# Products that keep TensorE at work across three stage boundaries, and two products moved ahead of a gate's, in a two-layer transformer kernel

## The reference

```python
x = x + ffn0(cond0(x, itok_B_0_8))   # adapter and layernorm chosen by language, then a quantised gated FFN
x = x + ffn1(cond1(x, itok_B_0_2))

def cond1(x, type_label):            # experts: one chosen by type, two shared
    s0, s1 = dense(x, swi[0], swo[0]), dense(x, swi[1], swo[1])
    eo = relu(x @ wi[type_label]) @ wo[type_label]
    gate_in = concatenate([eo[:, 0], s0[:, 0], s1[:, 0]])     # first token of each sequence
    w = softmax(relu(gate_in @ g1) @ g2)
    return eo * w[0] + s0 * w[1] + s1 * w[2]

def ffn1(x):                         # attention (16 heads), then a mixture of 8 experts, top 2
    x = x + attention(layernorm(x)) @ w_o + b_o
    h = layernorm(x)
    return x + mixture(h, top2(h @ gate_w + gate_b))
```

## Time and profile before

| | |
|---|---|
| median of 3 runs | 612.7 us (610.8 to 613.97) |
| the profiled execution | 612.18 us |
| its span, first to last instruction | 610.5 us |
| mean granted clock of PE | 0.966 |
| busy: PE, DVE, ACT, POOL | 536.3, 395.8, 375.2, 296.9 us |
| layer zero, typed experts, layer one begin on PE at | 2.36, 145.32, 216.72 us |

### The profile page before, as it was taken

How to read it: one execution, slowest core, us unless ns; L and a number is a source line. 1 busy time by engine, 2 the same in 40 slices (tenths; PEclk the granted TensorE clock), 3 DMA queues, 4 the chain that set the end, 5 groups by cost and what they waited for, 6 DMA issues and landing times.

```text
span 610.5 us, 18637 instructions
## 1 busy us (share of the span) xinstructions
PE 536.3 (88%) x5836; PEld 463.2 (76%) x5837; DVE 395.8 (65%) x1440; ACT 375.2 (61%) x799; POOL 296.9 (49%) x308
## 2 busy tenths in 40 slices
PE   6798998576999969899899998998988789999991
PEld 3555665366999958689788887887777688999991
DVE  5977788992433313367676876769866446668882
ACT  2366776884666523465546566466786477888870
POOL 1366777753000047442266836366476564555551
PEclk9999999997999969999999999999999799999996
DMA  8922999122333211020525202033322122236364
GB/s 280 376 48 77 400 401 392 57 73 82 107 104 102 77 39 40 23 53 20 170 51 183 71 20 59 20 74 83 78 63 59 50 75 64 72 89 197 86 195 134
DMA packets 75774, 70.81 MB, mean 116 GB/s; under 512 B 26802, under 2 KB 63012, under 8 KB 75300
## 3 DMA queue, kind: packets, MB, share of 16 engines
q1 hardware_dynamic: 67968, 55.34, 29.3%
q0 software_dynamic: 6400, 13.19, 6.6%
q10 hardware_dynamic: 1316, 1.15, 0.6%
HBM read 30.19 MB, written 39.46 MB: 114 GB/s over the span
## 4 chain that ended last, share of the span: by engine, by line
PE 44%; issue 6%; DVE 5%; POOL 5%; DMA 1%; DVEq 1%; ACT 1%; ACTq 0%; POOLq 0%
PE u_py L1712 7%; PE u_py L1874 6%; PE u_pz L1855 6%; PE u_pg L1855 3%; PE u_pf L1874 3%; PE u_pg L1755 2%; PE u_pz L1701 2%; PE u_pz L1703 2%; PE u_pz L1702 2%; PE u_pg L1763 2%; POOL rows_dram L1562 1%; PE u_pg L1777 1%; POOL u_eo_ew L1525 1%; PE u_pe L1727 1%; PE u_pf L1733 1%
## 5 line engine op out<-in xcount | busy, mean ns | idle before, releaser
L1572 POOL DMA_INDIRECT y_dram<-u_hh,v_to x71 | 68.1, 960 | 62.0 <-DVE u_hh L2645 49.7
L1562 POOL DMA_INDIRECT rows_dram<-u_row,u_slots x64 | 62.8, 981 | 46.8 <-DVE u_slots L2515 30.4
L1712 PE MATMUL u_py<-cwo,u_hh 128*128 128x128 f32 x512 | 68.5, 281 | 0.9 <-ACT u_hh L2097 0.7
L1712 PEld LDWEIGHTS u_py<-cwo,u_hh 128*128 128x128 f32 x512 | 63.5, 193 | 5.5 <-issue 2.5
L1874 PE MATMUL u_py<-w,v_h 128*128 x384 | 53.2, 282 | 7.1 <-DVE u_hh L2645 3.9
L1855 PE MATMUL u_pz<-v_xT,v_held 128*128 128x128 f32 x384 | 52.8, 283 | 4.8 <-DVE v_h L2625 4.2
L2097 ACT ACTIVATE u_hh<-u_pz 128x512 f32<-128x512 f32 x64 | 38.0, 596 | 28.0 <-PE u_pz L1703 25.0
L1874 PEld LDWEIGHTS u_py<-w,v_h 128*128 128x128 f32 x384 | 47.5, 194 | 9.9 <-issue 9.9
L1855 PEld LDWEIGHTS u_pz<-v_xT,v_held 128*128 128x128 f32 x384 | 48.2, 198 | 6.0 <-issue 4.7
L2170 ACT ACTIVATE v_held<-w 128x512 f32 x71 | 44.9, 633 | 11.8 <-PE u_pz L1855 3.6
L2177 ACT ACTIVATE v_h<-u_pz,p_bT 128x128 f32<-128x128 f32 x124 | 36.5, 368 | 12.4 <-PE u_pz L1855 10.4
(11 more groups left out here) (378 smaller groups left out, 1489.1 us busy)
## 6 DMA issues: line engine op xcount, KB each, us to landing
rows_dram<-zero SPq DMA_DIRECT2D x1, 17160.0 KB, 49.8
v_x<-rows_dram SPq DMA_DIRECT2D x71, 65.0 KB
w<-in_mw SPq DMA_DIRECT2D x2, 2048.0 KB
cwt<-in_cw SPq DMA_DIRECT2D x1, 2560.0 KB
xs_dram<-zero SPq DMA_DIRECT2D x1, 2240.0 KB, 12.6
e_xs<-xs_dram SPq DMA_DIRECT2D x35, 64.0 KB, 1.9
eo_dram<-e_y SPq DMA_DIRECT2D x35, 64.0 KB, 1.5
x_dram<-x SPq DMA_DIRECT2D x8, 256.0 KB
```

What stands on the lines that cost most here:

```text
L1562: pool.indirect_dma_start(rows_dram, bass.IndirectOffsetOnAxis(ap=slots[:, q, k, u:u + 1], axis=0), row[:, q, k, u, :], None).then_inc(sen ...
L1572: pool.indirect_dma_start(y_dram, bass.IndirectOffsetOnAxis(ap=vto[t % XR][:], axis=0), vy[:, t % XR, :], None).then_inc(v_sent[t % XR], 16)
L1712: last = nc.tensor.matmul(py[:, u * D:(u + 1) * D], hh[:, e % HR, u * P:(u + 1) * P], cwo[:, m * KF + k], start=(k == 0 and u == 0), stop= ...
```

## The change

In layer zero `first(2, 0)` and `first(2, 1)` stand ahead of `turn_rows(0)`; before, they stood between the first `up`s. At four places PE gets products whose results nobody reads: two of `zero` with 512 columns at the end of layer zero; three of the identity and typed weights with 256 columns at the start of the typed experts, into a bank that is written afterwards; two with 512 columns at their end; one with 512 columns in layer one, behind `turn_x(0)`. All are float32. In layer one `first(0, 0, 0)` and `first(0, 0, 1)` stand ahead of `gate(-1, 0)`, and `first(0, 0, 2)` ahead of `gate(-1, 1)`. In ScalarE's list `hidden(0, 0, 0)` stands ahead of its `gate(-1, 0)`. `gate` does nothing at any other i, and the order of the rest is the same.

```diff
                 second(1)
+                first(2, 0)
+                first(2, 1)
                 turn_rows(0)
                 up(0, 0)
-                first(2, 0)
                 up(0, 1)
-                first(2, 1)
                 first(2, 2)
...
                 turn_bias()
+                for n in range(2):
+                    nc.tensor.matmul(pg[:], zero[:, 0:P], zero[:, 0:INNER], start=True, stop=True)
...
+                def idle(bank, columns):
+                    nc.tensor.matmul(bank[:, 0:columns], ident[:], w1[:, 0:columns // D, :], start=True, stop=True)
+
+                for n in range(3):
+                    idle(py[0], 2 * D)
                 turn(0, 0, 0)
...
                 rolled(pe, step, TT, U, 1)
+                for n in range(2):
+                    idle(pT[0], FF)
...
+                    if i == -1:
+                        nc.tensor.matmul(py[:], ident[:], cwo[:, 0:SB, :], start=True, stop=True)
                     if ok(i - 2):
                         project(i - 2)
                     if ok(i):
                         first(i, 1, 3)
-                    gate(i, 0)
                     if ok(i):
                         second(i, 1, 2)
                     if ok(i + 1):
                         first(i + 1, 0, 0)
-                    gate(i, 1)
                     if ok(i):
                         second(i, 1, 3)
-                    gate(i, 2)
                     if ok(i + 1):
                         first(i + 1, 0, 1)
+                    gate(i, 0)
+                    if ok(i + 1):
                         first(i + 1, 0, 2)
+                    gate(i, 1)
+                    gate(i, 2)
...
-                    gate(i, 0)
                     if ok(i):
                         hidden(i, 1, 3)
                     if ok(i + 1):
                         hidden(i + 1, 0, 0)
+                    gate(i, 0)
```

## The result

The changed kernel took 607.27 us (median of 6 runs, 604.68 to 610.34), the kernel before beside it 613.07 (median of 6, 610.8 to 615.67). The ratio is 0.9924 with a 95% interval of 0.9896 to 0.9951: faster by 0.5 to 1.0%, by the ratio 4.7 us (the two medians lie 5.8 apart). The forecast was 608.6 with a range of 606.8 to 612.3. The profiled execution took 606.2 us, its span 604.5, against 612.18 and 610.5.

A forecast was written before the change was run, and what follows sets the result against it. TensorE was taken as busiest, slowed by 1.2 GHz stretches at three places, with engines waiting in turn in layer zero and early layer one. Three gains of 1.2 us, 3.6 in all, took 612.18 to 608.6 us; range 606.8 to 612.3.

The forecast's parts named there:

- Second edit: Typed experts' start: at full clock tile 0's `second` starts at 148.25 instead of 149.49; gain 1.2 us, bounds 0 and 1.5.
- Third edit: Layer one's start: `share(0)` comes sooner, so GpSimd's 1.30 us wait for `u_wtok` goes; gain 1.2 us, bounds -0.2 and 1.3.
- less the gathers' shift: Layer one: early firsts delay the gate, moving GpSimd's gathers by less than 0.2 us, taken off the 1.30 us gain.
- First edit: Layer zero: `second(2)` starts 1.4 us earlier and block 2's chain 1.2; gain 1.2 us, bounds 0 and 1.4.
- and the pipeline of layer zero with it: Layer zero: block 2's chain starts 1.2 us earlier, and the rest of the layer's pipeline moves forward with it.
- Cover at the barriers: Both barriers: GpSimd comes last, so 1.7 us of added products cost nothing, with 0.3 and 0.5 us of cover left.
- (a): Rival: the clock still falls, only somewhat later; one gain lost and another halved, 610.4 us; chance 0.31.
- (b): Rival: added products run at 1.2 GHz and hold up barriers and layer one; 615.8 us; chance 0.04.
- (c): Rival: products of zeros or the identity don't keep the clock; the order alone leaves about 612.3 us; chance 0.11.
- (d): Rival: transposes don't count as work for the clock, so the first boundary's 1.2 us is lost; 609.8 us; chance 0.04.
- Term 1: Layer zero: the gain of 1.2 us forecast for moving two firsts ahead of `turn_rows(0)`.
- terms 2 and 3: Typed experts' start and layer one's start: gains of 1.2 us forecast for each.

The follow-up runs named there:

- order_only: Changed kernel with both new orders and none of the added products: 610.23 us, ratio 0.9987 to the kernel before.
- starts_only: Changed kernel with the new orders and only the products behind the two barriers: 608.36 us, ratio 0.9947 to the kernel before.
- ends_only: Changed kernel with the new orders and only the products ahead of the two barriers: 609.58 us, ratio 0.9968 to the kernel before.
- products_only: Kernel before with all the added products, in the old orders: 606.77 us, ratio 0.9912 to the kernel before.
- before_w96: Kernel before with an already met TensorE wait repeated 42 times in layer zero (21 recorded instructions): 611.81 us, ratio 1.0012 to the kernel before.
- before_w32: Kernel before with an already met TensorE wait repeated 14 times in layer zero (7 recorded instructions): 612.39 us, ratio 1.0015 to the kernel before.
- doubled_ends: Changed kernel with four instead of two products ahead of each of the two barriers: 611.35 us, ratio 0.9999 to the kernel before.
- transposes: Changed kernel with every added product replaced by 128-column transposes taking the same time: 606.25 us, ratio 0.9896 to the kernel before.
- first_filled: `products_only` with two products of zeros ahead of `turn_rows(0)` and one before `up(0, 0)`: 610.28 us, ratio 0.9959 to the kernel before.
- filled: `first_filled` with further products in later gaps of layer zero and two ahead of `first_row(15)`: 609.7 us, ratio 0.9964 to the kernel before.
- after_w64: Changed kernel with an already met TensorE wait repeated 28 times in layer zero (14 recorded instructions): 605.33 us, ratio 0.9908 to the kernel before.
- after_w128: Changed kernel with an already met TensorE wait repeated 56 times in layer zero (28 recorded instructions): 608.91 us, ratio 0.9953 to the kernel before.

## Why the prediction was right, and where it was not

**Second edit, the typed experts' start: right.** 1.2 us were forecast; 1.14 came between the barrier and the first `e_y`. The size depends on how long the slow stretch lasts without the products: against the changed kernel, 0.9 to 1.1 us more in the kernel before and its two variants with waits, 2.3 to 2.4 in `order_only` and `starts_only`. The upper bound of 1.5, read from one execution, was too low for those. What the prediction didn't say is which products do it: those ahead of the barrier. The three behind it can be left out (`ends_only`, 6.31 us).

**Third edit, layer one: the size was right, the cause was wrong.** `u_nm` came 1.10 us sooner after the first gather (27.74 for 28.84), against 1.2. The prediction's step was that the two firsts, done ahead of the gate, bring `share(0)` forward. `order_only`, which has that order at 1.2 GHz, gains nothing (29.05); `products_only`, without it, gains 1.20 (27.64) and has its `weigh(0)` 0.3 us earlier than the changed kernel. The clock makes the gain, and the order costs about 0.3 us of GpSimd's gathers, as the prediction's "less the gathers' shift" has it. It depends on the execution, too: `before_w96`, which has neither products nor order, took 27.59 in its profile, where the clock fell for 6.8 us (216.4 to 223.2) and not for 10.2 as in before. A gain of 1.1 to 1.2 us is one against an execution with the long fall.

**First edit, layer zero: the term of 1.2 failed in its last step.** Block 2's chain did come forward, by 0.89 us from `l_xq` to the statistics (14.37 for 15.26), even though the clock fell at 31.8. But "and the pipeline of layer zero with it" did not hold. To the last scatter the distance is 113.2 us, as before, and the eight kernels with the new order average 113.1 against 112.8 for before, `before_w32`, `before_w96` and `products_only`. Nor does the order decide whether the clock falls near 30 us: it did in four of those eight profiles and in two of the other four. Where it did, block 2's chain took 15.3 to 15.4 us in the old order and 14.3 to 14.4 in the new; where it didn't, 13.9 and 13.7. Later the clock falls at other places of layer zero (45, 117 us), and these swallow the difference; why it falls at 117 us in one execution and not in another is open.

**Cover at the barriers: right.** Cover left of 0.3 and 0.5 us was forecast, and 0.2 and 0.5 is what the events show. Doubling gives the price beyond it, 1.63 and 1.31 us.

**The rivals.** (a), the clock falls somewhat later, happened at 31.8 and 222.9, and a fall at 117.1 came on top; at 222.9 it cost little, since GpSimd sets the pace there, and in layer zero the first edit's gain was lost. (b) didn't happen; `doubled_ends` shows its late barriers, though at full clock. (c) is refuted: with products ahead of the first barrier the clock stayed at 1.00 over it in all nine kernels that have them, and fell in all five without. (d) is refuted by `transposes`.

**The sum was right partly by luck.** Term 1 gave nothing net, terms 2 and 3 gave 2.2 us; averaged over the profiles of the table, the first three distances together are 149.5 us in before, its two variants and `order_only`, and 146.9 in the six kernels that have all four sets of products and no other fill: 2.7 us. The measured gain is 4.7. The forecast lacked some 2 us, which come in the rest of layer one, at places that it took to be only shifted. Averaged over the same profiles, the rest takes 361.1 us without the products and 359.8 with them; within each group it scatters by 4 to 5 us.

The number of breaks doesn't explain them, since the changed kernel has as much of this idle as before. What the two profiles show is where the lead changes. The idle of 1.70 us at 275 costs the changed kernel 2.0 us. The break of 2.52 us at 300, which only before has, and the clock at 0.50 for 3.4 us behind it (302.4 to 305.8) cost before 3.8. At 380 both have a break. Near 480 the clock of before is at 0.50 for 6.8 us, that of the changed kernel for 3.4, and the changed kernel gains another 2.3 or more. So both changes in its favour stand where the clock of before is slow for longer.

The clocks of all runs point the same way. In 90 runs of the kernel before, beside the experiments, the time falls as the mean clock rises (correlation -0.78), by 3.5 us for each 0.01. By this line the changed kernel, with 0.978 where before has 0.966, should be faster by 4.2 us, and its six runs lie 0.3 us under it, with a standard error of 0.9. This is a correlation, drawn beyond the clocks that before has, and it doesn't say where the time is won: in the two profiles 13.6 of the 15.2 us of slow clock that are gone lie at the two stage boundaries, which gave 2.2 us. But it sets other kernels apart. `doubled_ends`, with its late barriers, and `first_filled` and `filled`, with the longest idles (7.9 and 7.6 us), lie 2.6 to 3.3 us above the line. `after_w64`, with the shortest (3.3), lies 1.6 under it. `transposes` lies 2.3 under it with 5.2 us of idle and isn't explained.

What is shown, then: the products hold the clock and give all of the gain; an idle of this kind keeps its place in the stream; and the layout alone can move the median by 3 us (`after_w64` against `after_w128`). That layout is a part of this change's gain is not shown, and where the missing 2 us come from stays open. They vary between kernels whose boundaries are alike: `ends_only` is as short there as `products_only` (6.31 and 27.73 against 6.35 and 27.64), yet its ratio is 0.9968 against 0.9912, and its rest 364.4 us against 360.5.

## What to carry to other kernels

Products of constants ahead of a barrier that another engine reaches last are free as long as they end before that engine does, and they keep the clock for what follows; put them ahead of the wait (behind it they didn't help at the first barrier here), and measure the cover, since doubling them cost all that they had given. Credit such a gain only after running the products and the new order each by itself. A difference of half a percent in a kernel with groups of many small products can come from where the instructions happen to stand (two kernels that differ by 14 such instructions lay 3.6 us apart): run the same kernel with a few repeated waits before believing it, and count in the trace how many instructions these became. Note the granted clock of every run beside its time: here it tells more than the profile of one execution.

## What the runs showed of the hardware that was not expected

TensorE stands idle inside groups of small products at places fixed in its instruction stream, with one transfer of the instruction queue beside it: up to 2.5 us, at six places in layer one that the fourteen kernels have in common. Seven added instructions moved such a place by 4 products, 21 by 11, 28 by 14. That it has run out of instructions there is inferred from this, as the profile shows nothing else that it waits for. Behind a break of 2.32 us the clock was at 1.2 GHz for another 3.4 us.

Two repeated waits of one engine for a signal that has come are one instruction of 51 ns in TensorE's trace.

Products of zeros, products of the identity and transposes hold the clock alike: 6.25 to 6.39 us from the barrier to the first `e_y`, whichever they are.
